# Graph attention with residual and LayerNorm: half of the adjacency loads issued from ScalarE's DMA queue

## What is computed

```
in_fts = W @ x.T                          # W: 128 x 128, x: 4096 x 128
f1 = (w1 @ in_fts).T + b1                 # one number a node
f2 = (w2 @ in_fts).T + b2
logits = f1 + f2.T                        # 4096 x 4096
bias   = where(adj > 0, 0, -1e9)          # adj: 4096 x 4096 int32, 64 MB
coefs  = softmax(leaky_relu(logits) + bias, axis=-1)
out    = layernorm(x + coefs @ x, axis=-1)
```

## Time and profile before

| | |
|---|---|
| median of three runs | 393.35 us |
| span of the profiled execution | 391.8 us (no other time of that execution is given) |
| PE busy | 287.4 us (73%) |
| DVE busy | 285.5 us (73%) |
| ACT busy | 241.0 us (62%) |
| POOL busy | 105.7 us (27%) |
| DMA queue of SP (q1) | 25168 packets, 73.48 MB, 91.1% of the 16 DMA engines' span |
| DMA queue of ACT (q10) | 576 packets of 4 bytes |

### The profile page before, as it was taken

The page is one execution under the profiler, slowest core; times in us unless marked ns, Lnnn a source line. Parts: engine busy times, 40 slices in busy tenths (PEclk is TensorE's granted clock), DMA queues, the critical chain, the costliest instruction groups (busy, mean ns, idle before and its releaser), DMA issues.

```text
span 391.8 us, 5975 instructions
## 1 busy us (share of the span) xinstructions
PE 287.4 (73%) x2163; PEld 229.0 (58%) x2164; DVE 285.5 (73%) x415; ACT 241.0 (62%) x373; POOL 105.7 (27%) x83
## 2 busy tenths in 40 slices
PE   4779859691948876299819990999289936995492
PEld 3335538580846765288708880788168834884382
DVE  3769989827666575988397939693979388757994
ACT  2759986999293289625984498439861997010120
POOL 1744673005000040502050124004220414040641
PEclk9966968897996999599968997799869995999599
DMA  7999991999999999989999999999999999992001
GB/s 166 219 208 252 219 210 33 211 209 207 209 209 208 208 211 209 211 184 208 224 209 205 207 224 209 208 210 224 209 205 210 208 225 207 208 210 49 27 0 57
DMA packets 25762, 73.69 MB, mean 188 GB/s; under 512 B 3088, under 2 KB 7312, under 8 KB 25744
## 3 DMA queue, kind: packets, MB, share of 16 engines
q1 hardware_dynamic: 25168, 73.48, 91.1%
q10 hardware_dynamic: 576, 0.00, 0.1%
HBM read 71.37 MB, written 2.10 MB: 188 GB/s over the span
## 4 chain that ended last, share of the span: by engine, by line
DMA 60%; DVE 24%; issue 5%; SPq 5%; PE 2%; POOL 1%; DVEq 0%; POOLq 0%
DMA nat<-in_adj 59%; DVE mnt L593 11%; SPq L291 4%; DVE masks L608 3%; DVE post L585 2%; DVE masks L617 1%; POOL sgn L366 1%; DMA masks<-in_x 1%; DVE post L584 1%; SPq L285 1%; DVE mnt L599 1%; DVE ybt L771 1%; DVE rng L710 1%; PE ps L941 0%; PE ps L977 0%
## 5 line engine op out<-in xcount | busy, mean ns | idle before, releaser
L977 PE MATMUL ps<-bt,masks 128*128 128x258 f16 x2048 | 253.8, 289 | 85.1 <-DVE masks L608 85.0
L977 PEld LDWEIGHTS ps<-bt,masks 128*128 128x128 fp8e5 x2048 | 210.4, 103 | 128.3 <-issue 82.8
L447 ACT ACTIVATE sgn<-f1b,nf2l 128x512 int8<-128x512 f32 (+1 forms) x256 | 186.7, 852 | 2.2 <-DVE nf2l L646 1.6
L593 DVE TENSOR_SCALAR mnt<-nat 128x4096 fp8e5<-128x4096 int32 x32 | 76.2, 2384 | 83.2 <-DMA nat<-in_adj 83.1
L501 ACT ACTIVATE post<-ps,ac 128x258 f32<-128x258 f32 x64 | 26.5, 469 | 107.6 <-PE ps L977 107.6
L608 DVE SCALAR_TENSOR_TENSOR masks<-sgn,pat,mnt 128x256 uint32<-128x256 uint32 x128 | 67.8, 599 | 1.5 <-DVE mnt L599 1.4
L399 POOL TENSOR_TENSOR isox<-xsum,iso 128x516 f32<-128x516 f32 x7 | 17.9, 2557 | 140.5 <-DVE rec L761 140.5
L617 DVE SCALAR_TENSOR_TENSOR masks<-sgn,mnt 128x2048 uint32<-128x2048 uint32 (+2 forms) x18 | 42.2, 2346 | 0.0
L599 DVE STREAM_TRANSPOSE mnt<-mnt 128x1024 uint32<-128x1024 uint32 x32 | 37.9, 1220 | 0.0
L379 POOL TENSOR_TENSOR bt<-post,bt 128x1032 f16<-128x1032 f32 x8 | 22.3, 2782 | 18.8 <-ACT bt L462 18.8
L388 POOL TENSOR_TENSOR post<-post 128x1032 f32<-128x1032 f32 x7 | 17.8, 2539 | 24.7 <-ACT post L501 24.6
(11 more groups left out here) (85 smaller groups left out, 112.9 us busy)
## 6 DMA issues: line engine op xcount, KB each, us to landing
nat<-in_adj SPq DMA_DIRECT2D x128, 512.0 KB, 12.4
masks<-in_x SPq DMA_DIRECT2D x16, 128.0 KB, 4.6
out<-ybt SPq DMA_DIRECT2D x7, 256.0 KB, 16.0
out<-post SPq DMA_DIRECT2D x4, 64.0 KB, 2.3
wsb<-in_L_gnn_W SPq DMA_DIRECT2D x1, 64.0 KB, 2.3
w<-in_L_gnn_w ACTq DMA_DIRECT2D x2, 0.5 KB, 2.7
b<-in_L_gnn_b ACTq DMA_DIRECT2D x2, 0.5 KB, 3.6
xn<-in_x SPq DMA_DIRECT2D x1, 0.5 KB, 31.3
```

Source lines behind the costliest of these rows:

```text
L447: ins = act.activation(sgn_b[s][:, b, :, k], f1b[:, bass.ds(q * QW, QW)], ACT.Sign, bias=nf2l[:, n:n + 1], scale=-1.0)
L593: dve.tensor_scalar(mnt[:, 0, c * NK * P:(c + 1) * NK * P].bitcast(FP8), nat[:, c, :], 0, None, ALU.is_gt, saturate=False).then_inc(cast_d ...
L977: return pe.matmul(ps[:, 2 * c + m, 0:2 * DV], mask_f[slot][m][:, n // KB, n % KB, c * P:(c + 1) * P], btv[m][:, n, :], start=start, stop= ...
```

## The change

Quarters 2 and 3 (partitions 64 to 127) of x and of every adjacency row tile are issued by ScalarE on its own DMA queue. Quarters 0 and 1 stay on SyncE's. Both still add to the same semaphores, so VectorE waits for all four. ScalarE is a compute engine with its instructions in order, so its issues and their waits for `cast_done` take places among the activations: x and tiles 0 and 1 ahead of everything, tiles 2 and 3 in the start phase, tiles 4 and 5 ahead of quad 0, and then in quad q tiles 4q+6 and 4q+7 after the evacuation of tile 4q+1, and tiles 4q+8 and 4q+9 after that of tile 4q+3.

```diff
@@ SyncE
-                for a in range(A):
+                for a in range(A // 2):
                     sp.dma_start(xl[a * SQ:(a + 1) * SQ, :].rearrange("r (b n) -> r b n", b=NB)[:, two],
                                  x_cols[a][:, two]).then_inc(xl_in[h], 16)
             def load_adj(t, slot):
-                for a in range(A):
+                for a in range(A // 2):
@@ ScalarE
+            for h in range(BCH):
+                two = slice(h * NB // BCH, (h + 1) * NB // BCH)
+                for a in range(A // 2, A):
+                    act.dma_start(xl[a * SQ:(a + 1) * SQ, :].rearrange("r (b n) -> r b n", b=NB)[:, two],
+                                  x_cols[a][:, two]).then_inc(xl_in[h], 16)
+
+            def load_far(t, slot):
+                for a in range(A // 2, A):
+                    dst = nat[a * SQ:(a + 1) * SQ, slot, :].rearrange("s (g c) -> s g c", g=G)
+                    act.dma_start(dst, adj_v[t, a]).then_inc(nat_in[slot], 16)
+
+            load_far(0, 0)
+            load_far(1, 1)
...
                 split_x(i)
+                if i == BCH - 1:
+                    for t in (2, 3):
+                        act.wait_ge(cast_done, t - 1)
+                        load_far(t, t % 2)
...
-                def quad(q, s, more=True, share=(0, 3, 6, NB, NB)):
+                def load_pair(t):
+                    for c in range(2):
+                        act.wait_ge(cast_done, t + c - 1)
+                        load_far(t + c, c)
+
+                def quad(q, s, more=True, share=(0, 3, 6, NB, NB), ahead=2):
...
+                        if c == 1 and ahead:
+                            load_pair(QT * q + 6)
+                        if c == 3 and ahead == 2:
+                            load_pair(QT * q + 8)
...
+                load_pair(QT)
                 quad(0, 0, share=(0, 2, 2, 6, NB))
                 quad(1, 1)
                 with act.Fori(1, NQ // 2 - 1) as turn:
                     quad(2 * turn, 0)
                     quad(2 * turn + 1, 1)
-                quad(NQ - 2, 0)
-                quad(NQ - 1, 1, more=False)
+                quad(NQ - 2, 0, ahead=1)
+                quad(NQ - 1, 1, more=False, ahead=0)
```

## The result

The changed kernel takes 368.37 us (median of three runs, 368.26 to 371.64), the kernel before 393.35: a ratio of 0.940 (95% interval 0.935 to 0.946), 25 us less. The forecast was 380, with a range from 367 to 398. The measured time is inside that range, but not in the forecast's own band (374 to 386): it lies in that of the third rival (366 to 374).

The account below looks back on a forecast made before the run. The prediction took the loads, at 209 GB/s, to bound the kernel. Tile 7's cast at 118.0, plus 36.3 and five quads of 38.0 (190), put tile 31's at 344.3, 13.1 us sooner: 380 us, range 367 to 398.

Parts of the forecast that it names:

- third rival: ScalarE's issues: DMAs go out while earlier activations run, so a quad takes 36 us; 366 us in all, chance 0.17.
- rival of the columns: Loads of adj: paired quarters also differ in columns, which could explain the rate instead of halves; raised after the experiments, no chance.
- the middle of the bounds: Load rate with two queues: 250 GB/s, between 209 (no gain) and 292 (xn, which goes to all 128 partitions).
- The gate: Loop: ScalarE can't start the next quad's signs before the cast of tile 4q+7; a quad takes 38.0 us.
- four issues 2.0: ScalarE in each quad, behind the normalisation: four DMA issues charged at 0.5 us each, 2.0 us.
- the second sum: ScalarE's work from the cast of tile 4q+7 to the end of the next last signs: 29.7 us.
- A quad under 36.5: Loop in the profile after: a quad of 38 us was expected; under 36.5 would show that ScalarE's issues cost little.
- The first pairs: Before the loop: ScalarE's new waits delay the end of tile 7's cast from 113.4 to 118.0, 4.6 us lost.
- costed at nothing: Start: ScalarE's 12 more issues make its first copy 1.9 us late, against x's last chunk issued sooner; -2 to +2 us.
- The old rate (1): Loads: the two queues take turns at the old rate, quads stay at 40.7 us; 401 us, slower, chance 0.17.
- The small gain (2): Loads: about 222 GB/s, quads of 39 us because upper quarters come 1 us late; 388 us, chance 0.11.
- late upper quarters: Tiles 4q+10 and 4q+11: upper-quarter loads, issued late, just in time at 250 GB/s, about 1 us late at 222.

Follow-up runs that it names:

- the gate alone: The kernel before, all loads on SyncE's queue, with only ScalarE's waits for the casts added and no DMA of adj or x on ScalarE: 402.84 us, ratio 1.025.

## Why the prediction was right, and where it was off

**The bound before, and why 209 GB/s.** Right, and shown but for the rival of the columns named above: where a load lands limits it. Order alone, in one queue, gives 7 us; two queues in the same half give 209 GB/s; two queues in different halves 315. The Trainium skill, "SBUF — State Buffer", section 'Can I just issue two DMAs to hit both halves?', says that such DMAs serialize (+6%). The runs here don't agree: 50% more. Its ports ("Door 1: The DMA port swizzle") do agree with both the 209 and the loss of the same-half kernel.

**The rate.** I took 250, the middle of the bounds; it was 315, over the upper bound of 292, so xn was no ceiling. xn lands in rows of 512 bytes, an adjacency load in runs of 4 KB; whether that is why xn is slower wasn't tested. In the first pairs the cast of tile 5 starts 17.1 us behind the first issue, where 20.8 was predicted: 3.7 us.

**The gate.** Right in its place and nearly in its size: from the last sign to the end of the cast of tile 4q+7 8.6 us (8.2 predicted), from there to the next last sign 27.8 (29.7 predicted). The term that was mis-sized is "four issues 2.0" in the second sum: they cost nothing, as rival 3 had it. Against that the two issues behind the cast took 1.85 with their signal instead of 1.2; the activations themselves took 26.0 instead of 26.5. ScalarE sat idle 6.7 to 10.6 us at this place of each quad, 9.06 in the one shown; without the 1.85 of the issues this is 7.2 of waiting for the cast, where 6 to 7 was predicted. The five quads behind tile 11 took 36.2 each, not 38.0: 9 us. The one before took 34.0 instead of 36.3. A quad under 36.5 was one of the prediction's own signs of being wrong, and it came.

**The first pairs.** The cast of tile 7 was predicted for 118.0 and ended at 118.06, but not by the terms given: that it fits to 0.1 us is luck. The start lost 2.6 us (costed at nothing between -2 and +2), and the faster loads gained 3.7. From the cast of tile 5 to the last sign it took 18.9 us instead of 19.5, from there to the cast of tile 6 3.2 instead of 3.8, and the casts of tiles 6 and 7 took 6.97 us instead of 4.6. In the experiment with the gate alone they also took 6.97.

**The sum.** 13.1 us were forecast for the span and 25.3 measured. Of the 12.2 between them 11.2 are the six quads (226.3 predicted, 215.1 measured) and 1 the end behind the last cast (33.4 instead of 34.4 us). Nearly all of it is one error: I charged ScalarE 2.0 us a quad, 12 in six, for issues that run beside its activations, and gave the case in which they don't count 17%.

**Rivals.** The old rate (1) would have been 401; the gate alone gave 402.8 and the same-half kernel 406.1, so its price was right and its premise wrong. The small gain (2) was wrong in the rate. Rival 3 was right in the mechanism and near in the time: quads of 34.3 and 36 (34.0 and 36.2 measured) and 366 us. What spoke against it, late upper quarters, cost little: VectorE waited 13.0 us in all for tiles, at a rate over the 292 that rival 3 took.

## What to carry to other kernels

When loads go to a part of the partitions at a time, look at the rate where the part changes: a rise there speaks for the destination as the limit, though its size (217 to 219 GB/s here) says little about the gain (315). Then loads to different halves should be in flight at once; order alone, within one queue, gave 7 us. When a compute engine issues loads, price not the issues but the waits in front of them: what that engine has next in its program now depends on whoever frees the buffer. Put each such load behind the work after which its buffer is free anyway; here that was worth another 18 us behind the 25 of the change.

## What the runs showed that I had not expected

- Two queues on different halves moved 315 to 323 GB/s, more than one transfer to all 128 partitions before (292).
- Two queues on the same half moved 209 GB/s, the same as one.
- ScalarE issued DMAs 4 us and more ahead of activations that stand before them in its program: the issue at 240.41 is behind an evacuation that started at 244.31 and a normalisation that started at 245.02.
- The casts of tiles 6 and 7 took 6.97 to 7.00 us in every kernel in which they stood back to back, in place of the 4.48 to 5.35 of other such pairs; GpSimd worked on the sums of quad 0 then. That it is the cause wasn't tested.
